# Sixteen experts: the inverse deviation from a bit guess and Newton steps in place of a square root on ScalarE

## The reference, cut to what matters

```python
h = jnp.einsum('nc,ech->neh', x_flat, W1) + b1      # 4096 tokens, 16 experts, 128 hidden
mu = jnp.mean(h, axis=-1, keepdims=True)
var = jnp.mean(jnp.square(h - mu), axis=-1, keepdims=True)
h = (h - mu) * jax.lax.rsqrt(var + 1e-05) * g1 + be1
h = jax.nn.gelu(h, approximate=False)
expert_out = jnp.einsum('neh,eho->neo', h, W2) + b2
sel = jnp.take_along_axis(expert_out, topk_idx[:, :, None], axis=1)
y_flat = jnp.sum(sel * topk_w[:, :, None], axis=1)
```

## Time and profile before

| | |
|---|---|
| Time, median of 3 runs | 6295.27 us (6292.56 to 6296.06) |
| Profiled execution's own time | 6286.49 us |
| Its span, first to last instruction | 6284.7 us |
| Mean granted clock of TensorE | 0.96 of full |
| TensorE busy | 5601.0 us (89% of the span) |
| VectorE busy | 2978.1 us (47%) |
| ScalarE busy | 2475.4 us (39%) |
| GpSimd busy | 133.2 us (2%) |
| The 16-expert stage in the trace | 2385 to 2889 us after the start |

### The profile page before, as it was taken

How to read it: one execution, slowest core, us unless ns; L and a number is a source line. 1 busy time by engine, 2 the same in 40 slices (tenths; PEclk the granted TensorE clock), 3 DMA queues, 4 the chain that set the end, 5 groups by cost and what they waited for, 6 DMA issues and landing times. The chain is left out here.

```text
span 6284.7 us, 114370 instructions
## 1 busy us (share of the span) xinstructions
PE 5601.0 (89%) x38798; PEld 4322.7 (69%) x38989; DVE 2978.1 (47%) x8233; ACT 2475.4 (39%) x6283; POOL 133.2 (2%) x340
## 2 busy tenths in 40 slices
PE   7997699999999997889989988888888868888999
PEld 5773347788887775556757865687777848855666
DVE  3552322355554225663247743566666667543111
ACT  4442222233333225773224433355555535433333
POOL 1000000000000000000000000000000010000000
PEclk9999889999999998999989999899999989998999
DMA  0000000000000000000000000000000000000000
GB/s 33 0 0 18 0 18 0 0 1 0 0 0 7 0 0 0 0 0 24 0 0 1 0 3 0 1 1 2 2 1 2 1 39 0 0 0 0 0 0 13
DMA packets 2984, 26.62 MB, mean 4 GB/s; under 512 B 321, under 2 KB 833, under 8 KB 1473
## 3 DMA queue, kind: packets, MB, share of 16 engines
q1 hardware_dynamic: 2768, 23.76, 1.0%
HBM read 21.66 MB, written 2.10 MB: 4 GB/s over the span
## 5 line engine op out<-in xcount | busy, mean ns | idle before, releaser
L573 PE MATMUL banks<-clock_fill 128*128 128x512 bf16 x2509 | 695.5, 387 | 11.5 <-issue 1.1
L342 PE MATMUL banks<-attn_value,attn_probs_turned 128*128 128x144 f32 x3072 | 448.3, 289 | 0.7 <-ACT attn_probs_turned L402 0.2
L573 PEld LDWEIGHTS banks<-clock_fill 128*128 128x128 bf16 x2700 | 295.1, 113 | 214.3 <-issue 13.5
L623 PEld LDWEIGHTS banks<-act_a,weights 128*128 128x128 f32 x3048 | 399.2, 191 | 61.7 <-DVE act_a L669 7.6
L342 PE MATMUL banks<-cells_value,cells_probs_turned 128*128 128x136 f32 x3072 | 419.6, 280 | 0.2 <-ACT cells_probs_turned L402 0.2
L402 ACT ACTIVATE attn_probs_turned<-banks 128x512 f32<-128x512 f32 x384 | 229.6, 599 | 453.2 <-PE banks L331 453.1
L342 PEld LDWEIGHTS banks<-cells_value,cells_probs_turned 128*128 128x128 f32 x3072 | 397.8, 190 | 10.6 <-ACT cells_probs_turned L402 0.5
L342 PEld LDWEIGHTS banks<-attn_value,attn_probs_turned 128*128 128x128 f32 x3072 | 397.4, 190 | 5.7 <-ACT attn_probs_turned L402 2.0
L402 ACT ACTIVATE cells_probs_turned<-banks 128x512 f32<-128x512 f32 x384 | 229.6, 598 | 384.6 <-PE banks L331 384.6
L623 PE MATMUL banks<-act_a,weights 128*128 (+1 forms) x3048 | 375.0, 274 | 3.2 <-DVE act_a L669 3.2
L662 DVE TENSOR_TENSOR lstm_fc<-lstm_c,lstm_sig 128x32 f32<-128x32 f32 x384 | 73.8, 192 | 620.3 <-ACT lstm_sig L645 620.3
(11 more groups left out here) (403 smaller groups left out, 10644.2 us busy)
## 6 DMA issues: line engine op xcount, KB each, us to landing
weights<-in_p SPq DMA_DIRECT2D x1, 2894.5 KB, 16.1
weights<-in_p SPq DMA_DIRECT2D x1, 2894.0 KB, 9.6
weights<-in_p SPq DMA_DIRECT2D x2, 1364.0 KB, 8.5
x_res<-in_x SPq DMA_DIRECT2D x1, 2048.0 KB, 12.7
out_x<-x_res SPq DMA_DIRECT2D x1, 2048.0 KB, 6.3
weights<-in_p SPq DMA_DIRECT2D x1, 1836.0 KB, 11.0
weights<-in_p SPq DMA_DIRECT2D x1, 1835.5 KB, 7.0
weights<-in_p SPq DMA_DIRECT2D x1, 1344.5 KB, 9.7
```

Source lines behind the costliest of these rows:

```text
L342: last = pe.matmul(ps[:, CTX, bb * span:(bb + 1) * span], et[:, g, t * P:(t + 1) * P], vt[:, p, bb, h * span:(h + 1) * span], start=(g == ...
L573: pe.matmul(core.ps[:, FILL, :], core.fill[:, 0:P], core.fill[:, :], start=True, stop=True)
L623: last = pe.matmul(ps[:, first + parity, lo:lo + NB].unsqueeze(1), w("Wh", g * P, P), state, start=False, stop=True, skip_group_check=True)
```

## The change

The square root goes from ScalarE. In its place:

- `square` writes into tiles of 129 columns for each expert: 128 squares, now scaled so that they sum to the mean, and one column that holds 1e-5 (written once). The sum over 129 columns is the variance plus epsilon.
- `guess(a)` on VectorE, behind `sums(a, 3)` and ahead of `add(b, 0)`: two instructions on the bits of `var` (shift right by one, then 0x5F3759DF minus that) give a first value of 1/sqrt.
- `newton(a)` on GpSimd, behind the two copies of tile a: 13 instructions on 128x16 values, one product for half the variance and three rounds of four, nearly each of which waits for the one before it.
- `inverse(a)` on VectorE is now only the wait for GpSimd's result, at its old place ahead of `units(a, 0)`. `sums` gets a second wait, for the inverse of the tile before.
- `deviation(a)` and the reciprocal are gone.

```diff
--- before.py
+++ after.py
@@ -1381,14 +1381,17 @@
         ones = sb("ones", [3, P], mybir.dt.bfloat16)
         src = sb("src", [P, 2, P])
         g = sb("gate", [P, 2, NE])
-        sq = sb("square", [P, 2, CHUNK])
-        var, sd, inv = (sb(n, [P, NE]) for n in ("variance", "deviation", "inverse"))
+        sq = sb("square", [P, 2, 4, P + 1])
+        var, half_var, inv, part = (sb(n, [P, NE]) for n in ("variance", "half_variance", "inverse", "part"))
+        shifted = sb("variance_shifted", [P, NE], mybir.dt.int32)
+        steps = sb("newton_constants", [P, 2, NE])
         u = sb("units", [P, NQ, CHUNK])
         ht = sb("hidden_turned", [P, NQ, CHUNK])
         acc = sb("acc", [P, 4, P])
         s = {n: sem(n) for n in ["fold_done", "folded", "split", "rows_done", "rows_ready", "gates_turned",
                                  "gates_kept", "source_ready", "gate_ready", "h_done", "square_ready", "summed",
-                                 "sd_ready", "inv_ready", "unit_ready", "turn_done", "gelu_ready", "y_done", "y_added",
+                                 "eps_ready", "steps_ready", "shift_ready", "guess_ready", "newton", "inv_ready",
+                                 "unit_ready", "turn_done", "gelu_ready", "y_done", "y_added",
                                  "sum_done", "stored"]}
         block = ctx.enter_context(nc.Block())
 
@@ -1402,8 +1405,33 @@
             for k in range(NB, NB + 2):
                 body(*(Step(0, k - d, 2) if k - d < NB else None for d in range(3)))
 
+        NEWTON = 12
+
         @block.gpsimd
         def _(pool):
+            pool.memset(steps[:, 0, :], -0.5).then_inc(s["steps_ready"], 1)
+            pool.memset(steps[:, 1, :], 1.5).then_inc(s["steps_ready"], 1)
+            pool.wait_ge(s["steps_ready"], 2)
+
+            def newton(a):
+
+                at = a.n * NEWTON
+                pool.wait_ge(s["guess_ready"], a.n + 1)
+                past(pool, s["newton"], at)
+                pool.tensor_tensor(half_var[:, :], var[:, :], steps[:, 0, :], ALU.mult).then_inc(s["newton"], 1)
+                for r in range(3):
+                    pool.tensor_tensor(part[:, :], inv[:, :], inv[:, :], ALU.mult).then_inc(s["newton"], 1)
+                    pool.wait_ge(s["newton"], at + (4 * r + 2))
+                    pool.tensor_tensor(part[:, :], part[:, :], half_var[:, :], ALU.mult).then_inc(s["newton"], 1)
+                    pool.wait_ge(s["newton"], at + (4 * r + 3))
+                    pool.tensor_tensor(part[:, :], part[:, :], steps[:, 1, :], ALU.add).then_inc(s["newton"], 1)
+                    pool.wait_ge(s["newton"], at + (4 * r + 4))
+                    last = pool.tensor_tensor(inv[:, :], inv[:, :], part[:, :], ALU.mult)
+                    if r < 2:
+                        last.then_inc(s["newton"], 1)
+                        pool.wait_ge(s["newton"], at + (4 * r + 5))
+                last.then_inc(s["inv_ready"], 1)
+
             def body(a, b, c):
                 if a is None:
                     return
@@ -1411,6 +1439,7 @@
                 pool.tensor_copy(src[:, a.m, :], core.a[:, tok(a.n * P, P)]).then_inc(s["source_ready"], 1)
                 past(pool, s["y_added"], a.n * 4 - 4)
                 pool.tensor_copy(g[:, a.m, :].unsqueeze(1), gates[:, bass.ds(a.n, 1), :]).then_inc(s["gate_ready"], 1)
+                newton(a)
 
             run(pool, body)
 
@@ -1511,12 +1540,8 @@
             def square(a, q):
                 act.wait_ge(s["h_done"], a.n * 4 + (q + 1))
                 past(act, s["summed"], a.n * 4 + (q - 1))
-                act.activation(sq[:, q % 2, :], ps[:, q, :], ACT.Square).then_inc(s["square_ready"], 1)
-
-            def deviation(a):
-                act.wait_ge(s["summed"], a.n * 4 + 4)
-                act.activation(sd[:, :], var[:, :], ACT.Sqrt, bias=const("eps5"), scale=1.0 / P).then_inc(
-                    s["sd_ready"], 1)
+                act.activation(sq[:, q % 2, :, 0:P], ps[:, q, :].rearrange("p (e j) -> p e j", e=4), ACT.Square,
+                               scale=float(P) ** -0.5).then_inc(s["square_ready"], 1)
 
             def body(a, b, c):
                 for q in range(4):
@@ -1524,8 +1549,6 @@
                         gelus(b, q)
                     if a is not None:
                         square(a, q)
-                if a is not None:
-                    deviation(a)
                 if b is not None:
                     gelus(b, 3)
 
@@ -1535,6 +1558,8 @@
         def _(dve):
             wait_pack(dve, core, 3)
             dve.memset(ones[:, :], 1.0).then_inc(s["rows_ready"], 1)
+            dve.memset(sq[:, :, :, P:P + 1], 1.0e-5).then_inc(s["eps_ready"], 1)
+            dve.wait_ge(s["eps_ready"], 1)
             dve.wait_ge(s["fold_done"], NQ + 1)
             dve.tensor_copy(b1_left[:, 0, :], ps[:, TURN, 0:NE]).then_inc(s["folded"], 1)
             for q in range(NQ):
@@ -1555,12 +1580,20 @@
 
             def sums(a, q):
                 dve.wait_ge(s["square_ready"], a.n * 4 + (q + 1))
-                dve.tensor_reduce(var[:, q * 4:(q + 1) * 4], sq[:, q % 2, :].rearrange("p (e j) -> p e j", e=4), AX_X,
-                                  ALU.add).then_inc(s["summed"], 1)
+                past(dve, s["inv_ready"], a.n)
+                dve.tensor_reduce(var[:, q * 4:(q + 1) * 4], sq[:, q % 2, :, :], AX_X, ALU.add).then_inc(
+                    s["summed"], 1)
+
+            def guess(a):
+
+                dve.wait_ge(s["summed"], a.n * 4 + 4)
+                dve.tensor_scalar(shifted[:, :], var[:, :].bitcast(mybir.dt.int32), 1, None,
+                                  ALU.logical_shift_right).then_inc(s["shift_ready"], 1)
+                dve.wait_ge(s["shift_ready"], a.n + 1)
+                dve.tensor_scalar(inv[:, :].bitcast(mybir.dt.int32), shifted[:, :], -1.0, float(0x5F3759DF), ALU.mult,
+                                  ALU.add).then_inc(s["guess_ready"], 1)
 
             def inverse(a):
-                dve.wait_ge(s["sd_ready"], a.n + 1)
-                dve.reciprocal(inv[:, :], sd[:, :]).then_inc(s["inv_ready"], 1)
                 dve.wait_ge(s["inv_ready"], a.n + 1)
 
             def units(a, q):
@@ -1599,6 +1632,7 @@
                 if a is not None:
                     for q in range(1, 4):
                         sums(a, q)
+                    guess(a)
                 if b is not None:
                     add(b, 0)
                     add(b, 1)
```

## The result

The changed kernel takes 6436.44 us (median of 4 runs, 6399.5 to 6440.2) against 6293.92 of the kernel before (4 runs, 6287.35 to 6296.06): a ratio of 1.0215, with an interval of 1.0177 to 1.0253. The forecast was 6387, with a range of 6330 to 6445. A stage of layer 0 that the change doesn't touch took 54 to 58 us from its first to its last scaling in seven of the twelve profiled executions of this document and 86 to 91 in the other five, and the times of the two kernels fall into two groups each, some 33 us apart, which is the difference that the long stage makes.

A forecast was written before the change was run, and what follows sets the result against it. The stage was taken as bound by a ring through TensorE, the last square on ScalarE and VectorE's way to the units. A path of 46 us and a clock term of 46 us gave 92 us more, 6387 us, range 6330 to 6445.

The forecast's parts named there:

- a longer ring: Each pass's loop of TensorE, last square, VectorE's sums, adds and inverse, then TensorE again grows by 1.40 us; 46 us in all.
- ScalarE isn't on the ring: ScalarE's deviation is done 1.28 us before VectorE comes for it, so the 92 us of work taken away count nothing.
- The guess on VectorE: Two instructions ahead of `add(b, 0)`: guess ready 1.11 us after the last sum's start, the add at 1.03 instead of 0.60.
- The Newton chain: 13 dependent GpSimd instructions take 3.43 us; with the guess 4.54 us to `units(a, 0)` for 3.14, 1.40 us more a pass.
- The copy of `src`, now behind Newton: GpSimd's copy for the next tile comes after `newton(a)` but stays covered by 0.9 us before TensorE needs it.
- The first tile: It has no adds to cover the chain: 4.54 us from last sum to units instead of 1.91, 2.6 us more.
- TensorE's clock: Longer pauses at the end of a pass make nearly every pass lose the full clock once, one in seven twice: 46 us.
- The sum: Path 46 us plus clock 46 us make 92 us more, 6387 us against the median.
- The unchanged clock: Rival: TensorE's clock stays as it is and only the path grows by 46 us, 6341 us; chance 0.20.
- the hidden Newton: Rival: the Newton steps hide behind the adds, 5 us more, 6300 us, needing GpSimd at 0.14 us a step; chance 0.04.
- ScalarE: Rival: ScalarE sets the ring through `gelus(b, 3)` behind the second table load, 41 us gained, 6254 us; chance 0.03.
- The slow GpSimd: Rival: GpSimd takes 0.34 us a step and the clock falls for twice as long, 168 us more, 6463 us; chance 0.12.

The follow-up runs named there:

- e1: The changed kernel with products without use in TensorE's two pauses of each pass, 5 and 8 of them: 6345.12 us, ratio 1.0081 to the kernel before.
- e2: The kernel before with 3 products without use in each of TensorE's two pauses: 6285.26 us, ratio 0.9987 to the kernel before.
- e3: The kernel before with Square in place of Sqrt in the deviation, output of another function: 6303.00 us, ratio 0.9989 to the kernel before.
- e6: The changed kernel with the same 13 steps on VectorE, where it would wait for GpSimd: 6473.16 us, ratio 1.0265 to the kernel before.

## Why the prediction was right, and what it mis-sized

The two terms, a longer ring and a lower clock, are the right ones, and e1 and e2 separate them. Each was put too low, by 14 and 8 us.

- *ScalarE isn't on the ring.* Right: e3.
- *The guess on VectorE.* Right: ready 1.10 us after the start of the last sum, for 1.11 forecast. `add(b, 0)` starts 1.12 us after it in the middle of the passes, 1.21 in the one shown, for 1.03 forecast, and so TensorE's first pause is 1.27 to 1.37 us, where 0.75 + 0.4 was forecast.
- *The Newton chain.* Mis-sized: 1.40 us a pass were forecast, 1.83 measured, 57 us over the stage for 43. The step was put at 0.21 and a gap of 0.05; it is 0.22 and 0.08, 0.30 from start to start, and eleven times the 0.04 missing makes nearly all of the 0.43. Two smaller errors nearly cancel: the entry takes 0.17 us (2705.33 to 2705.50) for 0.05, and the second step needn't wait for the first and starts 0.18 us behind it for 0.26. The gap had come from a single wait behind a long memset, which was too little for a term that is taken so often. Groups of GpSimd after, to set beside the earlier trace rows:

```profile
L1425 POOL TENSOR_TENSOR experts_part<-experts_part,experts_half_variance 128x16 f32<-128x16 f32 x96 | 21.2, 221 | 7.5
L1421 POOL TENSOR_TENSOR experts_half_variance<-experts_variance,experts_newton_constants 128x16 f32<-128x16 f32 x32 | 7.1, 221 | 262.7 <-DVE experts_inverse L1593 262.7
```

- *The copy of `src`, now behind Newton.* Right: it ends at 2709.42 and the `hidden` that needs it starts at 2710.54.
- *The first tile.* 4.89 us to the units for 4.54 forecast, so 3.0 us more for 2.6; the path in all is 60 us for 46.
- *TensorE's clock.* The right mechanism, sized at 46 us and measured at 54. Every pass but the first lost the clock, as forecast; the stretch of double length came in 13 passes of 31, not in one of seven. The small share had been argued from the ten microseconds of unbroken work behind each pause, and the passes don't bear that out.
- *The sum.* 92 us forecast, some 115 measured with like runs, 142 in the first comparison, where the layer-0 stage adds some 30 that no step foresaw. With like runs the time would be some 6410 us, inside the forecast's range by its own terms. The 6436.44 measured lies in the range as well, but beyond the 6425 up to which the two terms were thought to reach, and that it is still in there is luck: about half of the miss of 49 us is of a stage that isn't part of the change.
- *Rivals.* The unchanged clock falls by e1, the hidden Newton by the 1.41 us wait, ScalarE by e3. The slow GpSimd had the right sign, at 0.30 us a step instead of 0.34. The hidden Newton was given a step of 0.14 us as its condition; by the prediction's own numbers, 3.30 - 1.11 - 0.10 us for 13 steps, 0.16 would have done, which 0.30 doesn't reach either.
- *VectorE as the better engine,* the rule of the Trainium skill's "GPSIMD Engine Reference", section 3.1, that the prediction weighed: the traces agree for the single step (0.21 against 0.30 us), and by e6 it is the wrong choice in this place.

## What to carry to other kernels

Work that leaves a busy engine is worth what stood in the ring: ask which wait ends last, and count the start-to-start time of each dependent small instruction, at its own engine's rate with its own wait. A pause that a change makes on TensorE costs twice where the clock is near falling: its own length, and the work behind it at half speed. And where an engine waits for a result, see first whether it is ready long before and only the consumer's order is late; here one add moved behind the units gave 35 us in the stage, 11 of them by the clock, and the root had never been in the way.

## What the runs showed of the hardware

- GpSimd's two-input instructions on 128x16 values take 0.22 us, and 0.30 from start to start where each waits for the one before; VectorE's take 0.17 and 0.21.
- With the long layer-0 stage TensorE was busy 99.4 of 101.0 us and had 0.56 of its clock, with the short one 65.7 of 67.0 at 0.85. So an engine that is 98% busy by the profile can still be granted about half of its clock for most of a stage. What sets it there was not tried; the windows from 800 us to the stage's end, before and after:

```profile
800.00:867.00 67.00, 65.71 (x110) 18.96 (x108) 16.53 (x24) 11.83 (x17) 0.00 (x0) 0.85 0.00 0
```

```profile
800.00:901.00 101.00, 99.41 (x112) 26.93 (x110) 16.58 (x25) 12.40 (x18) 0.00 (x0) 0.56 0.00 0
```
